# A ternary feed-forward: who clears, who rounds, and when the turned tile is copied

## The chip, the cores and the metric

The kernel runs on one core of a Trainium2 chip. The metric is the time on the device, in microseconds (us), of one execution of the whole program; a median over runs is given.

## The reference, cut to what matters

The program is a decoder of four layers on 2 x 1024 tokens of width 256, twelve sublayers, each `x = layernorm(x + sublayer(x))`. The change touches the third of them, a feed-forward with ternary weights and tokens rounded to eight bits:

```python
def _weight_quant(w):
    scale = 1.0 / jnp.clip(jnp.mean(jnp.abs(w)), 1e-05)
    return jnp.clip(jnp.round(w * scale), -1.0, 1.0) / scale
def _act_quant(x):
    scale = 127.0 / jnp.clip(jnp.max(jnp.abs(x), axis=-1, keepdims=True), 1e-05)
    return jnp.clip(jnp.round(x * scale), -128.0, 127.0) / scale
def _bitlinear(x, w):
    return jnp.einsum('bsi,oi->bso', _act_quant(x), _weight_quant(w))
gate = jax.nn.silu(_bitlinear(x, w_gate))      # 256 -> 1024
up = _bitlinear(x, w_up)                       # 256 -> 1024
return _bitlinear(gate * up, w_down)           # 1024 -> 256
```

The sublayer before it is a masked cross attention over 77 context tokens, the one behind it a paged causal attention.

## The kernel before, in words

Each sublayer is a stage, a block of five instruction streams, one for each engine, written in order by hand and joined by semaphores; all engines meet at a barrier between stages. The tokens are held twice on chip: x_tok with tokens on partitions (16 tiles of 128 tokens) and xT turned.

The ternary stage is `bit_ffn_stage` (L1122). Its start-up: TensorE takes the mean of the absolute weights (summed in the stage before); VectorE makes the scales. Rounding to whole numbers is done by adding a large constant (ROUND, 1.5 x 2^23) and taking it away again. For weights, `weight(n)` on ScalarE does both (L1258 adds, L1260 takes away and casts to bf16), and `clip(n)` on VectorE clips to -1 and 1 (L1335). For tokens, `quant_x(c)` on VectorE takes a group of four tiles: maximum (L1320), m127 (L1322), reciprocal (L1324), four scalings with the constant added (L1330); `quant_x(c)` on ScalarE takes the constant away and casts (L1266); `turn_x(c)` on TensorE turns the group by eight transposes into a half of h_ps; `copy_x(c)` on ScalarE copies it to xqT (L1270). All four groups are done before the loop. sx, the scale of the tokens times that of the weights, is made once for all tiles (L1361).

The loop runs over the 16 tiles n, with two rounds more to run out. TensorE: gate(n+1) into g_ps (L1196), upward(n+1) into u_ps (L1205), downward(n-1) into y_ps (L1222), turn_h(n), eight transposes into h_ps (L1214), and, from round 11 on, a turned tile of the normalized output (`tail.turn`, L3002). ScalarE: silu(n+1) of g_ps (L1276), copy_h(n-1), which takes the constant away from all of h_ps and casts to hqT (L1289), round_h(n), which scales the hidden tile and adds the constant (L1282), and a small scaling; from round 11 on the copy of a turned output tile (L3009). VectorE: hidden(n), which is the product of silu and u_ps (L1342), its maximum (L1344), and two small steps to the scale of the rounding; each second round the residual of two tiles with its statistics (`tail.add`, L2939, L2948, L2952), and at rounds 10, 14, 17 and 18 the norm of the tiles that are ready (L2982). Waits: gate(n+1) needs silu(n) done, upward(n+1) needs the product of hidden(n), turn_h(n) needs round_h(n) and copy_h(n-1), copy_h(n) needs turn_h(n), downward(n) needs copy_h(n).

GpSimd fills v_all, the values of the paged attention (128 x 8192 f32, 4 MB), with zero (L1168), waits, and sets the columns of ones (L1170); later it takes the roots for the norms. The first stage of the program uses v_all's room for products of its own; the second stage, `masked_heads_stage` (L863), does not. In the second stage SyncE's queue issues the loads of the three ternary weights (`bit.load`) and then `clear_outputs`, a DMA that clears 4 MB of token_outputs in the main memory from a tile of zeros; the experts' stages wait for it, far later.

## Time and profile before

| what | us |
|---|---|
| plain runs, median of 3 | 2783.19 (2782.19 to 2787.72) |
| profiled execution | 2797.71 |
| span of its trace | 2795.6 |
| stage before (masked cross attention) | 263.36 to 413.46 |
| ternary stage | 413.46 to 541.99 |
| TensorE busy over the span | 2461.0 (88%) |
| VectorE / ScalarE / GpSimd busy | 1451.2 / 885.6 / 507.1 |

PE is TensorE's products, PEld its weight loads, DVE VectorE, ACT ScalarE, POOL GpSimd, SP SyncE. A timeline row gives the start and the length in us, engine, line, operation, written tile<-read tiles, shapes and count; in square brackets stands how long the engine had been idle before it, and who ended that. A row of several instructions (x4) gives the time from the first to the last. A row of the table of stretches gives from:to, length, the busy time of each engine with its count, TensorE's granted clock as a share of 2.4 GHz, the share of the DMA engines and GB/s. A row of the groups gives count | busy us, mean ns of one | idle us before.

### The profile page before, as it was taken

What the parts mean: (1) busy time and instruction counts of PE and PEld (TensorE: products, weight loads), DVE (VectorE), ACT (ScalarE), POOL (GpSimd) and SP (SyncE); (2) the same over time, 40 slices, a digit from 0 to 9 for tenths busy, and PEclk for the clock granted to TensorE, in tenths of its full rate; (3) what the DMA queues carried; (4) which work ended last, traced back from release to release, by engine and by line L of the source; (5) the groups of instructions that cost most, each with busy time, mean ns of one, the idle gap of its engine ahead of it and who ended that gap; (6) DMA issues with size and microseconds to landing.
All of it is one profiled execution on the core that took longest, in us unless ns stands there. A gap on an engine that the chain in (4) does not pass through costs nothing. (4 is left out here: it accounts for less than half of the span.)

```text
span 2795.6 us, 35763 instructions
## 1 busy us (share of the span) xinstructions
PE 2461.0 (88%) x14243; PEld 1700.6 (61%) x14251; DVE 1451.2 (52%) x2493; ACT 885.6 (32%) x1293; POOL 507.1 (18%) x424
## 2 busy tenths in 40 slices
PE   6887775778888979988999998979999799999888
PEld 4665663432222768865667666756666577777764
DVE  7996876558774440125564564561110355455543
ACT  1111556424556113324432442211221222222132
POOL 3332340040001123420100001112221310001010
PEclk8898887988999979999999999869999899999999
DMA  3002000054330025633322321132231300000000
GB/s 111 1 1 78 29 22 9 8 129 88 63 63 26 14 86 216 236 111 106 96 73 56 95 66 33 30 119 67 100 100 57 107 18 17 12 12 17 1 33 30
DMA packets 73542, 177.23 MB, mean 63 GB/s; under 512 B 16919, under 2 KB 37016, under 8 KB 67833
## 3 DMA queue, kind: packets, MB, share of 16 engines
q1 hardware_dynamic: 60484, 122.54, 15.5%
q0 software_dynamic: 10368, 50.01, 5.3%
q10 hardware_dynamic: 2542, 2.62, 0.3%
q8 instruction: 103, 1.69, 0.3%
q14 instruction: 45, 0.37, 0.0%
HBM read 149.51 MB, written 25.43 MB: 63 GB/s over the span
## 5 line engine op out<-in xcount | busy, mean ns | idle before, releaser
L1623 PE MATMUL L_ffn_h_ps<-L_ffn_xgT,L_ffn_w 128*128 128x512 f32 (+2 forms) x992 | 231.9, 390 | 7.0 <-DVE L_ffn_xgT L1706 3.4
L1635 PE MATMUL L_ffn_y_ps<-L_ffn_w,L_ffn_h 128*128 128x256 f32 x1008 | 222.5, 380 | 4.8 <-issue 3.9
L526 DVE TENSOR_REDUCE L_attn_neg<-L_attn_Y 128x1 f32<-128x512 f32 (+3 forms) x304 | 187.3, 658 | 55.3 <-PE L_attn_Y L399 53.9
L1681 ACT ACTIVATE L_ffn_h<-L_ffn_h_ps,L_ffn_w 128x640 f32<-128x640 f32 (+2 forms) x184 | 101.9, 555 | 346.7 <-PE L_ffn_h_ps L1623 333.4
L1635 PEld LDWEIGHTS L_ffn_y_ps<-L_ffn_w,L_ffn_h 128*128 128x128 f32 x1008 | 189.7, 190 | 33.1 <-issue 8.3
L1623 PEld LDWEIGHTS L_ffn_h_ps<-L_ffn_xgT,L_ffn_w 128*128 128x128 f32 x992 | 154.2, 192 | 84.1 <-issue 66.8
L496 ACT ACTIVATE L_attn_room<-L_attn_Y 128x1024 f32<-128x1024 f32 (+1 forms) x192 | 147.6, 814 | 80.5 <-PE L_attn_Y L450 79.8
L399 PE MATMUL L_attn_Y<-L_attn_K,L_attn_Q 104*128 104x512 bf16 (+3 forms) x384 | 119.5, 362 | 43.4 <-DVE L_attn_neg L526 26.0
L1715 DVE TENSOR_TENSOR L_ffn_yg<-L_ffn_y_ps,L_ffn_w 128x256 f32<-128x256 f32 x63 | 26.8, 425 | 223.5 <-PE L_ffn_y_ps L1635 223.5
L1706 DVE COPY L_ffn_xgT<-L_ffn_t_ps 128x256 f32<-128x256 f32 x63 | 24.6, 421 | 214.2 <-PE L_ffn_t_ps L1610 195.3
L1756 POOL DMA_INDIRECT token_outputs<-L_ffn_yg,puts x63 | 62.0, 984 | 325.6 <-DVE L_ffn_yg L1715 325.6
L2330 PE MATMUL L_attn_X<-xT,L_attn_w 128*128 128x512 f32 x256 | 113.0, 594 | 0.0
L2330 PE MATMUL L_attn_X<-xT,L_attn_first_w 128*128 128x512 f32 x256 | 112.8, 593 | 0.0
L399 PEld LDWEIGHTS L_attn_Y<-L_attn_K,L_attn_Q 104*128 104x128 bf16 x384 | 33.6, 100 | 117.1 <-DVE L_attn_neg L526 95.7
L2878 POOL TENSOR_TENSOR L_attn_prod<-L_attn_k_sum,L_attn_qs 128x1024 f32<-128x1024 f32 x16 | 37.7, 2356 | 347.9 <-DVE L_attn_qs L2852 347.9
L844 POOL TENSOR_TENSOR L_attn_v_all<-L_attn_q,L_attn_kv 128x2048 f32<-128x2048 f32 x16 | 73.9, 4623 | 132.9 <-DVE L_attn_room L802 59.8
L450 PE MATMUL L_attn_Y<-L_attn_Q,L_attn_K 107*128 107x512 bf16 (+3 forms) x384 | 95.9, 335 | 2.0 <-ACT L_attn_room L496 1.9
L2556 POOL TENSOR_TENSOR L_attn_sq_sum<-L_attn_sq_sum,L_attn_sq 128x1024 f32<-128x1024 f32 x14 | 33.0, 2359 | 331.1 <-ACT L_attn_sq L2433 331.1
L2415 ACT ACTIVATE L_attn_bc<-L_attn_bc 128x1024 f32<-128x1024 f32 x32 | 33.9, 1059 | 172.2 <-DVE L_attn_bc L2508 172.2
L435 PE MATMUL L_attn_Y<-L_attn_room,L_attn_v_all 128*32 128x512 f32 (+3 forms) x768 | 83.0, 511 | 0.1
L2330 PEld LDWEIGHTS L_attn_X<-xT,L_attn_w 128*128 128x128 f32 x256 | 47.8, 192 | 53.8 <-issue 53.8
L2330 PEld LDWEIGHTS L_attn_X<-xT,L_attn_first_w 128*128 128x128 f32 x256 | 47.3, 190 | 53.9 <-issue 53.1
(578 smaller groups left out, 5065.7 us busy)
## 6 DMA issues: line engine op xcount, KB each, us to landing
L_ffn_w<-in_L_ffn_w SPq DMA_DIRECT2D x8, 2180.0 KB
L_attn_bc<-decays SPq DMA_DIRECT2D x32, 512.0 KB, 6.1
L_attn_bp<-decays SPq DMA_DIRECT2D x32, 256.0 KB, 6.9
L_attn_Q<-L_attn_q_parts SPq DMA_DIRECT2D x48, 128.0 KB, 4.3
L_attn_K<-L_attn_k_parts SPq DMA_DIRECT2D x48, 128.0 KB, 6.4
L_attn_first_w<-in_L_attn_w SPq DMA_DIRECT2D x8, 640.0 KB
L_attn_w<-in_L_attn_w SPq DMA_DIRECT2D x8, 640.0 KB, 3.9
token_outputs<-zero SPq DMA_DIRECT2D x1, 4096.0 KB, 21.2
```

The costliest lines, as they stand in the source:

```text
L399: mm = nc.tensor.matmul(R[n % 2][:, u * wdt:(u + 1) * wdt], Q[0:KM, par, j0 + u, tt * P:(tt + 1) * P], K[0:KM, par, j0 + u, c * CW:c * CW ...
L435: mm = nc.tensor.matmul(O[32 * j:32 * j + 32, lo:CW], v_all[:, it, gt, 32 * j:32 * j + 32], probs[:, (2 * n + j // 2) % 4, j % 2, lo:CW], ...
L450: mm = nc.tensor.matmul(S[e % 2][:, j % 2, lo:CW], K[0:KS, par, j, gt * P:(gt + 1) * P], Q[0:KS, par, j, tc * CW + lo:(tc + 1) * CW], star ...
L496: nc.scalar.activation(probs[:, e % 4, :, lo:CW], S[e % 2][:, :, lo:CW], ACT.Exp, scale=SCALE).then_inc(exp_done, 1)
L526: nc.vector.tensor_reduce(neg[:, c, j0:j0 + heads, tt], R[n % 2][:, 0:heads * width(tt, c)].rearrange("p (h k) -> p h k", h=heads), X_AXIS ...
L844: nc.gpsimd.tensor_tensor(prod[n % 2][:, h, :, :], q[n % 2][:, h, :].unsqueeze(2).broadcast_to([P, HALF, H, DH]), keys(n).unsqueeze(1).bro ...
L1623: ins = nc.tensor.matmul(h_ps[f % 2][:, lo // CW, 0:hi - lo], w1[g % NB][:, kt, f * P:(f + 1) * P], xgT[u][:, kt, lo:hi], start=kt == 0, s ...
L1635: ins = nc.tensor.matmul(y_ps[k % 2][:], h[:, f, t * P:(t + 1) * P], w2[g % NB][:, f, :], start=f == 0, stop=f == FT - 1)
L1681: nc.scalar.activation(h[:, f, 0:n], h_ps[f % 2][:].rearrange("p c n -> p (c n)")[:, 0:n], func, bias=b1[g % NB][:, f:f + 1]).then_inc(sem ...
L1756: nc.gpsimd.indirect_dma_start(core.outputs, at, yg[g % 2][:, t, :], None).then_inc(y_stored[g % 2], 16)
L2330: ins = nc.tensor.matmul(x[:, c * CW:(c + 1) * CW], w[1 - par][:, kt, r, :], xT[:, kt, b * T + c * CW:b * T + (c + 1) * CW], start=kt == 0 ...
L2878: nc.gpsimd.tensor_tensor(prod[:], k_sum[:], qs[1 - par][:], ALU.mult).then_inc(prod_ready, 1)
```

## The change

Five things. The zeros of v_all are written by a DMA on SyncE's queue in the stage before, between the weights' loads and `clear_outputs`; GpSimd waits for it where it filled. Of each token group, `scale_x` (maximum, m127, reciprocal, and now that group's sx) and `round_x` (scaling with the constant, and the subtraction of it with the cast to bf16) are both on VectorE; group 0 comes before the loop, groups 1 to 3 are spread over rounds 1, 2, 4, 6 and 8; turning and copying them follow in rounds 2, 6 and 10, through x_ps in place of h_ps. For weights, VectorE takes the constant away and clips in two passes. ScalarE's table of silu is loaded by an activation of one column, ahead of the first silu. And copy_h(n-1) stands before silu(n+1), in two halves of four transposes each, each with its own signal.

```diff
@@ masked_heads_stage, sync
             bit.load(sp)
+            flat = values[:].rearrange("p i t n -> p (i t n)").rearrange("p (a n) -> p a n", n=2 * P)
+            sp.dma_start(flat, over(core.zero[:], flat.shape[1])).then_inc(bit.values_cleared, 16)
             clear_outputs(core, sp)
@@ bit_ffn_stage
-        xq_ps = [h_ps[:, 4 * u:4 * u + 4, :].bitcast(BF16).rearrange("p a (b n) -> p (a b n)", b=2) for u in range(2)]
+        xq_ps = x_ps[:].bitcast(BF16)
+        HALF = FT // 2
+        TURN_X = {2: 1, 6: 2, 10: 3}
+        SCALE_X, ROUND_X = {1: 1, 2: 2, 6: 3}, {1: 1, 4: 2, 8: 3}
@@ gpsimd
-            nc.gpsimd.memset(values[:], 0.0).then_inc(v_cleared, 1)
-            pool.wait_ge(v_cleared, 1)
+            pool.wait_ge(weights.values_cleared, 16)
@@ tensor
             def turn_h(n):
                 pe.wait_ge(h_up, n + 1)
-                if n:
-                    pe.wait_ge(hqT_ready, n)
-                for ft in range(FT):
-                    mm = nc.tensor.transpose(h_ps[:, ft, :], hr[n % 2][:, ft * P:(ft + 1) * P], core.ident[:])
-                mm.then_inc(h_turned, 1)
+                for half in range(2):
+                    if n:
+                        pe.wait_ge(hqT_ready, 2 * n - 1 + half)
+                    for ft in range(half * HALF, half * HALF + HALF):
+                        mm = nc.tensor.transpose(h_ps[:, ft, :], hr[n % 2][:, ft * P:(ft + 1) * P], core.ident[:])
+                    mm.then_inc(h_turned, 1)
             def downward(n):
-                pe.wait_ge(hqT_ready, n + 1)
+                pe.wait_ge(hqT_ready, 2 * n + 2)
...
             gate(0)
-            turn_x(1)
             pe.wait_ge(w_clipped, 2)
             upward(0)
-            turn_x(2)
-            turn_x(3)
-            pe.wait_ge(xqT_ready, N // P // QT)
             for n in range(NT_ + 2):
                 if n + 1 < NT_:
                     gate(n + 1)
                     upward(n + 1)
+                if n in TURN_X:
+                    turn_x(TURN_X[n])
@@ scalar
             def copy_h(n):
-                act.wait_ge(h_turned, n + 1)
                 if n >= 4:
                     act.wait_ge(tail.y_mm, (n - 2) // 2)
-                nc.scalar.activation(hqT[n % 2][:], h_ps[:], ACT.Identity, bias=down_[:]).then_inc(hqT_ready, 1)
+                for half in range(2):
+                    act.wait_ge(h_turned, 2 * n + half + 1)
+                    ft = slice(half * HALF, half * HALF + HALF)
+                    nc.scalar.activation(hqT[n % 2][:, ft, :], h_ps[:, ft, :], ACT.Identity, bias=down_[:]).then_inc(hqT_ready, 1)
             weight(0)
-            quant_x(0)
+            weight(1)
             copy_x(0)
-            weight(1)
-            for c in range(1, N // P // QT):
-                quant_x(c)
-                copy_x(c)
-            act.wait_ge(sx_set, 1)
+            nc.scalar.activation(warm[:], core.one[:], ACT.Silu)
             silu(0)
             weight(2)
             for n in range(NT_ + 2):
+                if 1 <= n <= NT_:
+                    copy_h(n - 1)
                 if n + 1 < NT_:
                     silu(n + 1)
-                if 1 <= n <= NT_:
-                    copy_h(n - 1)
+                if n in TURN_X:
+                    copy_x(TURN_X[n])
                 if n < NT_:
                     round_h(n)
@@ vector
+            def scale_x(c):
...
+                for k in range(2):
+                    last = nc.vector.tensor_scalar(sx[:, k, t], m127[:, t], wmean[:, k:k + 1], None, ALU.mult)
+                last.then_inc(sx_set, 1)
+            def round_x(c):
...
+                dve.wait_ge(x_up, c + 1)
+                nc.vector.tensor_scalar(xq[c % 2][:], xr[c % 2][:], -ROUND, None, ALU.add).then_inc(x_down, 1)
             def clip(n):
+                dve.wait_ge(w_up, n + 1)
+                nc.vector.tensor_scalar(wq[n][:], w32[n][:], -ROUND, 1.0, ALU.add, ALU.min).then_inc(w_down, 1)
                 dve.wait_ge(w_down, n + 1)
-                nc.vector.tensor_scalar(wq[n][:], wq[n][:], 1.0, -1.0, ALU.min, ALU.max).then_inc(w_clipped, 1)
+                nc.vector.tensor_scalar(wq[n][:], wq[n][:], -1.0, None, ALU.max).then_inc(w_clipped, 1)
...
-            quant_x(0)
-            quant_x(1)
+            scale_x(0)
+            round_x(0)
             clip(0)
-            quant_x(2)
             clip(1)
-            quant_x(3)
...
             for n in range(NT_ + 2):
                 if n < NT_:
                     hidden(n)
+                if n == 0:
+                    clip(2)
+                if n in SCALE_X:
+                    scale_x(SCALE_X[n])
+                if n in ROUND_X:
+                    round_x(ROUND_X[n])
```

## Rows read from the trace of the kernel before

**Rows 1.** Table of stretches: the stage before, the middle of the loop, everything behind.
```profile
263.36:413.46 150.10, 114.67 (x1264) 95.73 (x1264) 118.61 (x151) 78.25 (x150) 53.40 (x47) 0.86 0.15 50
455.00:510.00 55.00, 39.78 (x247) 23.99 (x251) 41.98 (x80) 36.30 (x43) 1.92 (x2) 1.00 0.00 1
541.99:2795.60 2253.61, 2059.72 (x11753) 1408.36 (x11753) 1029.40 (x1999) 683.87 (x966) 351.83 (x332) 0.94 0.24 71
```

**Rows 2.** Timeline of the ternary stage, its start-up: start us, us, engine, line.
```profile
413.46 6.92 POOL L1168 MEMSET L_attn_v_all<- 128x8192 f32 x1 [2.22 <-POOLq L57]
...
414.30 2.10 ACT L1258 ACTIVATE L_ffn_w<-L_ffn_w,L_ffn_round_up,L_ffn_wscale 128x2048 f32<-128x2048 f32 x1 [0.34 <-DVE L_ffn_wscale L1353]
...
415.40 5.00 DVE L1322 TENSOR_SCALAR L_ffn_m<-L_ffn_amax 128x4 f32<-128x4 f32 x1
...
421.81 1.21 DVE L1320 TENSOR_REDUCE L_ffn_amax<-x_tok 128x4 f32<-128x1024 f32 x1
...
423.47 1.14 DVE L1330 TENSOR_SCALAR L_ffn_xr<-x_tok,L_ffn_ascale 128x256 f32<-128x256 f32 x4
...
424.27 1.01 ACT L1270 COPY L_ffn_xqT<-L_ffn_h_ps 128x1024 bf16<-128x1024 bf16 x1 [1.19 <-PE L_ffn_h_ps L1186]
...
432.67 0.37 DVE L1361 TENSOR_SCALAR L_ffn_sx<-L_ffn_m,L_ffn_wmean 128x16 f32<-128x16 f32 x2
...
438.42 1.28 ACT L1276 ACT_TABLE_LOAD   x1
...
444.95 0.69 DVE L1335 TENSOR_SCALAR L_ffn_wq<-L_ffn_wq 128x2048 bf16<-128x2048 bf16 x1 [11.90 <-ACT L_ffn_wq L1260]
...
445.56 1.28 DVE L1342 SCALAR_TENSOR_TENSOR L_ffn_h<-L_ffn_u_ps,L_ffn_sx,L_ffn_sg 128x1024 f32<-128x1024 f32 x1
...
451.57 1.06 PE L1196 MATMUL L_ffn_g_ps<-L_ffn_wq,L_ffn_xqT 128*128 128x512 bf16 x2
...
453.27 1.81 PE L1205 MATMUL L_ffn_u_ps<-L_ffn_wq,L_ffn_xqT 128*128 128x512 bf16 x4
```

**Rows 3.** Timeline, one round in the middle of the loop.
```profile
470.43 1.11 ACT L1289 ACTIVATE L_ffn_hqT<-L_ffn_h_ps,L_ffn_round_down 128x1024 bf16<-128x1024 f32 x1
...
470.57 1.28 DVE L1342 SCALAR_TENSOR_TENSOR L_ffn_h<-L_ffn_u_ps,L_ffn_sx,L_ffn_sg 128x1024 f32<-128x1024 f32 x1 [2.37 <-ACT L_ffn_sg L1276]
...
471.43 1.24 ACT L1282 ACTIVATE L_ffn_hr<-L_ffn_h,L_ffn_round_up,L_ffn_hscale 128x1024 f32<-128x1024 f32 x1
...
472.72 0.85 PEld L1214 LDWEIGHTS L_ffn_h_ps<-ident,L_ffn_hr 128*128 128x128 f32 x8 [0.36 <-ACT L_ffn_hr L1282]
...
473.41 0.88 DVE L2939 SCALAR_TENSOR_TENSOR x_tok<-L_ffn_y_ps,L_ffn_sh,x_tok 128x256 f32<-128x256 f32 x2
...
474.71 1.12 ACT L1276 ACTIVATE L_ffn_sg<-L_ffn_g_ps,L_ffn_sx 128x1024 f32<-128x1024 f32 x1 [1.86 <-PE L_ffn_g_ps L1196]
...
475.10 0.25 DVE L2952 BATCH_NORM_AGGREGATE L_ffn_tail_mv<-L_ffn_tail_stats 128x2 f32<-128x6 f32 x2
```

**Rows 4.** Timeline, a round with a turned output tile, and the stage's end.
```profile
519.98 1.24 ACT L1282 ACTIVATE L_ffn_hr<-L_ffn_h,L_ffn_round_up,L_ffn_hscale 128x1024 f32<-128x1024 f32 x1
...
521.96 1.37 DVE L2982 TENSOR_SCALAR x_tok<-x_tok,L_ffn_tail_mv,L_ffn_tail_rstd 128x256 f32<-128x256 f32 x4
...
522.84 0.59 ACT L3009 COPY xT<-L_ffn_x_ps 128x512 f32<-128x512 f32 x1 [1.44 <-PE L_ffn_x_ps L3002]
...
533.41 1.12 ACT L1289 ACTIVATE L_ffn_hqT<-L_ffn_h_ps,L_ffn_round_down 128x1024 bf16<-128x1024 f32 x1
...
534.59 0.77 PEld L1222 LDWEIGHTS L_ffn_y_ps<-L_ffn_wq,L_ffn_hqT 128*128 128x128 bf16 x8 [1.93 <-ACT L_ffn_hqT L1289]
...
541.99 0.50 PEld L251 LDWEIGHTS L_attn_Y<-xT,L_attn_room 128*128 128x128 f32 x2 [1.94 <-issue]
```

**Rows 5.** DMA issues of the page: KB, us to landing.
```profile
token_outputs<-zero SPq DMA_DIRECT2D x1, 4096.0 KB, 21.2
```

**Rows 6.** Groups by line and shape on VectorE.
```profile
L2092 DVE TENSOR_SCALAR L_router_hit_all<-L_router_g,L_router_cand 128x1024 bf16<-128x1024 f32 x7 | 5.3, 753 | 0.2
```

More of the change, by code:

```diff
@@ L860, in _, with masked_heads_stage @@
                     tail.shift(pool, g)
-def masked_heads_stage(nc, core, early, bit):
+def masked_heads_stage(nc, core, early, bit, values):
     A = core.A
@@ L1258, in weight @@
                 nc.scalar.activation(w32[n][:], w32[n][:], ACT.Identity, scale=wscale[:, n:n + 1], bias=up[:]).then_inc(w_up, 1)
-                act.wait_ge(w_up, n + 1)
-                nc.scalar.activation(wq[n][:], w32[n][:], ACT.Identity, bias=down_[:]).then_inc(w_down, 1)
-            def quant_x(c):
-                act.wait_ge(x_up, c + 1)
-                if c >= 2:
-                    act.wait_ge(xq_turned, c - 1)
-                nc.scalar.activation(xq[c % 2][:], xr[c % 2][:], ACT.Identity, bias=down_[:]).then_inc(x_down, 1)
             def copy_x(c):
                 act.wait_ge(xq_turned, c + 1)
-                nc.scalar.copy(xqT[:, :, c * QT * P:(c + 1) * QT * P], xq_ps[c % 2].rearrange("p (k n) -> p k n", k=KT)).then_inc(xqT_ready, 1)
+                nc.scalar.copy(xqT[:, :, c * QT * P:(c + 1) * QT * P], xq_ps).then_inc(xqT_ready, 1)
             def silu(n):
                 act.wait_ge(g_mm, n + 1)
+                act.wait_ge(sx_set, n // QT + 1)
                 if n >= 2:
@@ L1327, in quant_x @@
                     dve.wait_ge(x_down, c - 1)
+                    dve.wait_ge(xq_turned, c - 1)
                 for k in range(QT):
@@ L1353, in _ @@
             nc.vector.reciprocal(wscale[:], wmean[:]).then_inc(w_scaled, 1)
-            quant_x(0)
-            quant_x(1)
+            scale_x(0)
+            round_x(0)
             clip(0)
-            quant_x(2)
             clip(1)
-            quant_x(3)
-            for k in range(2):
-                last = nc.vector.tensor_scalar(sx[:, k, :], m127[:], wmean[:, k:k + 1], None, ALU.mult)
-            last.then_inc(sx_set, 1)
-            dve.wait_ge(sx_set, 1)
-            clip(2)
             for n in range(NT_ + 2):
@@ L3050, in __init__ @@
         self.summed = nc.alloc_semaphore("L0_ffn_w_summed")
+        self.values_cleared = nc.alloc_semaphore("L0_ffn_values_cleared")
     def load(self, sp):
```

15 lines of the change are left out of this document (7 added, 8 removed).

## The prediction, made before the changed kernel ran

> **What bounds the kernel now.** I read the table of stretches first, then the timeline of the stage that the change touches, line by line. TensorE is busy for 2059.7 of the 2253.6 us behind this stage [rows 1], and nothing is changed there; what counts is how much earlier the ternary feed-forward ends. The stage runs from 413.46 us [rows 2] to 541.99, where the first product of the next stage begins. The reader is to see three parts in it.
>
> Start-up, 413.46 to 445.56, where VectorE begins the first gated product, "hidden(0)" [rows 2]. TensorE isn't the limit here. GpSimd's fill of v_all takes 6.92 us and ends at 420.38; VectorE's two-step operation on four numbers (L1322) begins at 415.40 and ends at 420.40, 5.00 us, though the whole group of maximum, L1322 and reciprocal takes 421.81 to 423.47 = 1.66 us once the fill is over. So the fill holds it up by some 4.8 us. After that ScalarE does everything: all casts, all copies, a table load of 1.28 at 438.42, the third weight; VectorE stands idle for 11.90 us until its clip at 444.95 [rows 2].
>
> The loop, one token tile per round. Starts on ScalarE show the round: silu 474.71, copy of the turned tile 1.01 later (as each 128x1024 step passes on after about 1.0: copy 470.43, rounding 471.43), rounding 1.00 later, TensorE's turn of h 1.29 after the rounding's start (472.72), next silu 1.99 later. 1.01 + 1.00 + 1.29 + 1.99 = 5.29 us [rows 3]. It is a ring through ScalarE and TensorE; VectorE's part of it (hidden 470.57, next operation 473.41: 2.84) isn't in the ring. Output tiles turned from unit 11 on make it longer.
>
> The end: after the last copy (533.41) the down product follows at 534.59, and the next stage 7.40 after that [rows 4].
>
> **Part 1: the clear by DMA.** The fill goes; GpSimd waits for a DMA issued at the start of the stage before, which lasts 150 us [rows 1]. The nearest row is the clear of token_outputs, also 4 MB, from the same zero tile: 21.2 us to landing, behind 3 MB of weights [rows 5]. Bounds: nothing, or, if writing into the on-chip memory were twice as slow, some 45 us, which still ends 100 us before the feed-forward. It delays the clear behind it, which nobody wants before the experts. I take 0. If the cover were gone, GpSimd would wait, and behind it only the ones and the roots of the norm, first needed near 475. Gain on the path: 4.8 us, in the start-up below.
>
> **Part 2: start-up.** VectorE passes 415.40 as before. Then m127 and reciprocal 1.66 - 1.25 = 0.41 (the maximum's 1.21 and 0.04 of hand-over), two scalings of sx 0.34 (0.37 measured for 16 columns), four roundings 1.14 and a wait of 0.05, and the subtraction. The last, f32 to bf16, 128x1024, isn't done by this stage now; the same form elsewhere takes 0.75 [rows 6], and the other bound is the maximum's full-rate 1.21 [rows 2]. I take 0.75, since kind of operation and shapes are the same. 415.40 + 0.41 + 0.34 + 1.19 + 0.75 = 418.09. ScalarE's copy follows a finished cast by 1.19 and takes 1.01: 420.29; gate(0) 420.4. I leave TensorE at 1.2 GHz there, as it is in these rows now (512 columns in 0.43 us): gate to upward 453.27 - 451.57 = 1.70, upward 1.81 [rows 2].
> The clips: f32 to bf16 over 2048 columns plus a second pass, which is today's 0.69 and passes on after 0.61 [rows 2]. First pass: twice 0.75 less one fixed part, 1.4 (bounds 1.3 and 2.4); 2.04 each. Clip(0) ends at 420.1, clip(1) at 422.2; ScalarE has the two weights scaled by 414.30 + 2 x 2.10 = 418.5. So upward(0) starts at 422.2, not 422.1, and hidden(0) at 422.2 + 1.81 + 0.1 = 424.1. The table load is done ahead, between 420.3 and the silu at 422.5; without that cover it would cost 1.3. Start-up gains 445.56 - 424.1 = 21.5 us.
>
> **Part 3: what bounds the loop afterwards.** The copy now stands before the silu. The ring then has no copy in it: rounding 1.29, turn and gate 1.99, silu 1.01 = 4.29, and the half copies fit while gate works. But VectorE has taken on work and becomes the bound of units 0 to 10. Its sum from hidden(0) to hidden(11) [rows 2 to 4, 6]:
> 11 x hidden 2.84 = 31.2; clip(2) 2.0; three scale_x at 1.66 + 0.34 = 6.0; three round_x at 1.19 + 0.75 - 0.07 (overlap) = 5.6; four residual additions with statistics, 473.41 to 475.35 less 0.08 overlap, 1.86 each = 7.4; the norm of eight tiles, 2 x 1.37 - 0.1 = 2.6. Together 54.9 us, 4.99 a unit, under 5.29 but well over 4.29. The waits in between hold: from the end of hidden(n-1) the ring needs 1.29 + 1.99 + 1.15 (1.01 and 470.57 - 470.43) = 4.43 us to hidden(n+1), and VectorE has 2.84 plus the extra steps of two units, at least 3.7, to do in that time. The copies of turned tokens (1.0 each, three times) fall in this slack of 2.1 us. Were they to stick out, they would cost 1.0 each.
>
> From unit 11 the extra steps end and the turned output tiles begin, so ScalarE is the bound. From a rounding's start: output tile's copy 519.98 to 522.84 = 2.86, then that copy 0.59 less 0.11 overlap, two half copies, silu 1.01. A half copy of 128x512: between the 0.48 of the 128x512 output copy and half of 1.00 plus a whole fixed part, 0.65; I take 0.57, the 0.48 plus what a biased activation takes over a copy at 1024 columns (1.11 against 1.01). Round: 2.86 + 0.48 + 1.14 + 1.01 = 5.49. In the rest, hidden(11) to its scale 2.92; three rounds 16.5; from rounding 14 to rounding 15 without a silu 4.48; then 2.86 + 0.48, the second half 0.57 later, its 0.68 and 0.06 of hand-over to the down product (1.31), and 7.40. Sum from hidden(0): 54.9 + 2.9 + 16.5 + 4.5 + 12.0 = 90.8 us against 541.99 - 445.56 = 96.4 now [rows 2, 4]. Gain 5.6.
>
> The half copies are the one edit with a price: as a whole the copy passed on after 1.00, in halves after 1.14. The Trainium skill (ScalarE: Activation LUTs, What ACT_TABLE_LOAD costs) gives a biased ACTIVATE 280 ns + 0.833 ns a column, 93 ns of it overlapped with the next: 1.13 whole, which agrees with the 1.11 of the row, and 2 x 0.61 for the halves. By it each late round would be 0.09 longer and the whole gain smaller by an estimated 0.4 us.
>
> **Sum.** 21.5 + 5.6 = 27.1 us. The profiled execution took 2797.71 us (span 2795.6), the median of the plain runs is 2783.19, 14.5 less; I carry the difference over unscaled: 2756.1 us, and 2770.6 under the profiler.
>
> **Rivals.**
> (a) The loop gives nothing. VectorE's sum needs only 5.6 us more, 0.47 for each of the 12 extra steps before hidden(11), and each holds a wait on its own engine, which I cost at 0.03 to 0.05. Against: the rows of the group 421.81 to 423.47 hold three such waits already. Gain 21.5: 2761.7.
> (b) The converting operations run at full rate, not double: 0.46 + 2 x 1.0 in the start-up, 1.0 + 3 x 0.46 in the loop, 4.8 together. Gain 22.3: 2760.9. The same number comes out if the 5.00 us of L1322 isn't the fill's doing, which the two ends within 0.02 us speak against.
> (c) Slower: TensorE never gets to 2.4 GHz in this stage. Its work is then the bound: gate and upward 1.70 each [rows 2], turn twice the 0.85 of [rows 3], and as much for down, also eight products: 6.8 a unit. hidden(15) comes at 424.1 + 15 x 6.8 + 8 for turned tokens and output tiles = 534, the end 4.5 + 12 and some 3 for the slower products later, 554: 12 us late, 2795. It decides where the granted clock is near 0.5 for most of the loop. For it: 512 columns still take 0.43 us at 453, with idle gaps at each wait [rows 2]. Against: 1.00 over 455 to 510 with TensorE busy for 39.8 of 55 us [rows 1], and the new loop has less idle time for the same work. The Trainium skill (TensorE: Matmul & The Clock Gate, Part 1) holds that half rate is the default and that activity releases it; gaps speak for this rival, but by that rule, too, the denser loop should stay at the upper level, and the trace agrees for the present gaps.
> (d) The stages behind run at another mean clock: 0.01 of the 0.94 there is 2059.7 x 0.0106 = 22 us [rows 1]. It has no sign; the plain runs lie within 5.5 us of each other, so I give it a few us at both ends.
>
> **Chances.** The forecast 0.74, its own range 2751 to 2761 (unknown costs: conversions, half copies, 0.5 us of clock in the start-up, and (d)); (a) 0.10; (b) with its twin 0.08; (c) 0.03; (d) as the decider 0.05. The range takes in (a) and (b) and 5 us of drift: 2749 to 2768. About 0.2%, 5.6 us, is what can be told from no change. Faster 0.93, within 0.04, slower 0.03.
>
> **What would show it.** Right: L1322's successor takes 0.17 us; the first hidden starts near 424; VectorE idles hardly at all between then and hidden(11), near 479; rounds of about 5.0 there, 5.5 from unit 11; the turned tile's copies of about 0.68 us each; the next stage starts near 515. Wrong: the subtraction near 1.2; VectorE idle in the first eleven units (then the ring or TensorE's order bounds); granted clock at 0.5 behind 430; or a next stage that starts near 515 while the total isn't 27 us shorter, which would put the difference behind this stage.

## The result, and the profile after

| comparison | kernel before, us | changed kernel, us | ratio, 95% interval |
|---|---|---|---|
| first | 2785.28 (2782.19 to 2794.69) | 2768.39 (2764.22 to 2772.95) | 0.9934, 0.9913 to 0.9955 |
| second | 2786.29 (2778.60 to 2796.22) | 2762.27 (2760.21 to 2770.25) | 0.9915, 0.9890 to 0.9939 |
| third | 2789.60 (2783.97 to 2797.12) | 2759.37 (2754.66 to 2760.80) | 0.9891, 0.9875 to 0.9907 |

The change makes the kernel faster, by 0.7 to 1.1 per cent: by 16.9 us in the comparison that the prediction is held against, by 24.0 and 30.2 in two later ones. The forecast was 27.1. The profiled execution took 2769.68 us (span 2767.9) against 2797.71 and 2795.6: 28.0 and 27.7 less. Times are medians.

The table of stretches of the changed kernel: the stage before, the whole ternary stage, as much of its loop as rows 1 show, everything behind the stage.

```profile
263.02:413.30 150.28, 114.98 (x1264) 96.08 (x1264) 118.63 (x151) 78.33 (x150) 53.46 (x47) 0.86 0.23 78
413.30:514.06 100.76, 68.18 (x442) 43.62 (x450) 83.68 (x178) 74.91 (x98) 5.62 (x9) 0.94 0.06 21
425.00:480.00 55.00, 41.64 (x278) 26.80 (x284) 53.22 (x109) 44.10 (x59) 1.93 (x2) 1.00 0.00 1
514.06:2767.90 2253.84, 2060.84 (x11753) 1410.76 (x11753) 1028.09 (x1999) 682.63 (x966) 351.77 (x332) 0.94 0.24 71
```

The stage runs from 413.30 to 514.06. It ends 27.93 us earlier than before, and what lies behind takes 2253.84 us where it took 2253.61 [rows 1]: in these two traces all of the gain is made in the stage and all of it stays. In 55 us of the loop TensorE is busy for 41.64 us, where it was for 39.78 [rows 1], and VectorE for 53.22, where it was for 41.98. The stage before takes 150.28 us with the second clear in it and took 150.10 [rows 1]. The clear of v_all is issued at 264.34 and lands 22.0 us later, 127 us ahead of the ternary stage: its cover holds, as forecast.

The start-up, beside rows 2:

```profile
414.14 4.08 ACT L1260 ACTIVATE L_ffn_w<-L_ffn_w,L_ffn_round_up,L_ffn_wscale 128x2048 f32<-128x2048 f32 x2 [0.35 <-DVE L_ffn_wscale L1359]
...
415.24 0.17 DVE L1317 TENSOR_SCALAR L_ffn_m<-L_ffn_amax 128x4 f32<-128x4 f32 x1
...
416.95 0.69 DVE L1334 TENSOR_SCALAR L_ffn_xq<-L_ffn_xr 128x1024 bf16<-128x1024 f32 x1
417.56 1.22 DVE L1338 TENSOR_SCALAR L_ffn_wq<-L_ffn_w 128x2048 bf16<-128x2048 f32 x1
...
418.84 1.01 ACT L1264 COPY L_ffn_xqT<-L_ffn_x_ps 128x1024 bf16<-128x1024 bf16 x1 [0.62 <-PE L_ffn_x_ps L1190]
...
420.68 0.69 DVE L1340 TENSOR_SCALAR L_ffn_wq<-L_ffn_wq 128x2048 bf16<-128x2048 bf16 x1
...
421.65 1.91 PE L1208 MATMUL L_ffn_u_ps<-L_ffn_wq,L_ffn_xqT 128*128 128x512 bf16 x4
...
423.71 1.28 DVE L1348 SCALAR_TENSOR_TENSOR L_ffn_h<-L_ffn_u_ps,L_ffn_sx,L_ffn_sg 128x1024 f32<-128x1024 f32 x1 [2.34 <-PE L_ffn_u_ps L1208]
```

GpSimd no longer fills; VectorE's two-step operation takes 0.17 us where it took 5.00 [rows 2]. The subtraction (L1334) takes 0.69, a weight's first pass 1.22 and its second 0.69. ScalarE has scaled two weights by 418.22 and then waits for the turned tokens. The first gated product starts at 423.71, 10.4 us after the stage's start, where it was 32.1 [rows 2].

Two units in the middle of the loop, beside rows 3. The first ends with a residual addition (L2944 and its statistics), the second with a group's rounding (L1331, L1334):

```profile
442.23 0.88 DVE L2944 SCALAR_TENSOR_TENSOR x_tok<-L_ffn_y_ps,L_ffn_sh,x_tok 128x256 f32<-128x256 f32 x2
...
444.11 1.28 DVE L1348 SCALAR_TENSOR_TENSOR L_ffn_h<-L_ffn_u_ps,L_ffn_sx,L_ffn_sg 128x1024 f32<-128x1024 f32 x1
...
444.83 1.27 ACT L1286 ACTIVATE L_ffn_hqT<-L_ffn_h_ps,L_ffn_round_down 128x512 bf16<-128x512 f32 x2 [0.56 <-PE L_ffn_h_ps L1218]
...
446.13 1.11 ACT L1271 ACTIVATE L_ffn_sg<-L_ffn_g_ps,L_ffn_sx 128x1024 f32<-128x1024 f32 x1
...
446.98 1.14 DVE L1331 TENSOR_SCALAR L_ffn_xr<-x_tok,L_ffn_ascale 128x256 f32<-128x256 f32 x4
...
448.15 0.69 DVE L1334 TENSOR_SCALAR L_ffn_xq<-L_ffn_xr 128x1024 bf16<-128x1024 f32 x1
...
448.76 1.28 DVE L1348 SCALAR_TENSOR_TENSOR L_ffn_h<-L_ffn_u_ps,L_ffn_sx,L_ffn_sg 128x1024 f32<-128x1024 f32 x1
```

VectorE is never idle in these rows: 442.23 to 444.11 is the addition, 1.88 us, and from the hidden tile at 444.11 to the next it is 4.65. ScalarE is the one that waits now. The copy of the turned tile (L1286, two halves) comes at 444.83, ahead of the silu at 446.13.

A late round and the end, beside rows 4:

```profile
486.45 1.26 ACT L1277 ACTIVATE L_ffn_hr<-L_ffn_h,L_ffn_round_up,L_ffn_hscale 128x1024 f32<-128x1024 f32 x1
...
489.32 0.59 ACT L3014 COPY xT<-L_ffn_x_ps 128x512 f32<-128x512 f32 x1 [1.44 <-PE L_ffn_x_ps L3007]
...
489.80 1.27 ACT L1286 ACTIVATE L_ffn_hqT<-L_ffn_h_ps,L_ffn_round_down 128x512 bf16<-128x512 f32 x2
...
490.95 1.12 ACT L1271 ACTIVATE L_ffn_sg<-L_ffn_g_ps,L_ffn_sx 128x1024 f32<-128x1024 f32 x1
...
491.95 1.25 ACT L1277 ACTIVATE L_ffn_hr<-L_ffn_h,L_ffn_round_up,L_ffn_hscale 128x1024 f32<-128x1024 f32 x1
...
514.06 0.50 PEld L251 LDWEIGHTS L_attn_Y<-xT,L_attn_room 128*128 128x128 f32 x2 [1.95 <-issue]
```

From rounding to rounding 5.50 us: 2.87 to the output tile's copy, 0.48, then 1.15 for the two halves and 1.00 for the silu. ScalarE isn't busy throughout: 1.44 of the 2.87 are its wait for TensorE's turn of the output tile. It is the order of its queue that makes the round.

The groups of both kernels over their stages show the two waits that the change removes. Columns: busy us, mean ns of one, then the idle time before them and who ended it. Before:

```profile
L1342 DVE SCALAR_TENSOR_TENSOR L_ffn_h<-L_ffn_u_ps,L_ffn_sx,L_ffn_sg 128x1024 f32<-128x1024 f32 x16 | 20.5, 1284 | 20.5 <-ACT L_ffn_sg L1276 16.7 <-PE L_ffn_u_ps L1205 3.8
...
L1276 ACT ACTIVATE L_ffn_sg<-L_ffn_g_ps,L_ffn_sx 128x1024 f32<-128x1024 f32 x16 | 17.8, 1115 | 23.1 <-PE L_ffn_g_ps L1196 23.1
```

and after:

```profile
L1348 DVE SCALAR_TENSOR_TENSOR L_ffn_h<-L_ffn_u_ps,L_ffn_sx,L_ffn_sg 128x1024 f32<-128x1024 f32 x16 | 20.5, 1281 | 5.8 <-ACT L_ffn_sg L1271 2.8 <-PE L_ffn_u_ps L1208 2.3 <-issue 0.7
L1286 ACT ACTIVATE L_ffn_hqT<-L_ffn_h_ps,L_ffn_round_down 128x512 bf16<-128x512 f32 x32 | 20.3, 687 | 7.4 <-PE L_ffn_h_ps L1218 7.4
...
L1271 ACT ACTIVATE L_ffn_sg<-L_ffn_g_ps,L_ffn_sx 128x1024 f32<-128x1024 f32 x16 | 17.9, 1116 | 0.7 <-PE L_ffn_g_ps L1199 0.5
```

Silu waited 23.1 us for the gate products and waits 0.7; VectorE's wait ahead of the hidden tile fell from 20.5 to 5.8, which lies in the first unit and in the late ones.

### The profile page after: what moved, and what is told of

Same layout as the page of the kernel before. It is cut to its first block and busy times, and to the rows that moved or that the text cites. A ratio compares the mean times of both kernels' runs of the same rounds, so it can differ in the third digit from the quotient of the medians.

```text
span 2767.9 us, 35799 instructions
## 1 busy us (share of the span) xinstructions
PE 2455.5 (89%) x14243; PEld 1701.9 (61%) x14251; DVE 1450.8 (52%) x2506; ACT 877.6 (32%) x1303; POOL 500.1 (18%) x423
## 5 line engine op out<-in xcount | busy, mean ns | idle before, releaser
L1628 PEld LDWEIGHTS L_ffn_h_ps<-L_ffn_xgT,L_ffn_w 128*128 128x128 f32 x992 | 154.9, 193 | 83.9 <-issue 67.8
L2335 PEld LDWEIGHTS L_attn_X<-xT,L_attn_first_w 128*128 128x128 f32 x256 | 47.3, 190 | 53.9 <-issue 53.1
## 6 DMA issues: line engine op xcount, KB each, us to landing
L_attn_Q<-L_attn_q_parts SPq DMA_DIRECT2D x48, 128.0 KB, 4.2
L_attn_K<-L_attn_k_parts SPq DMA_DIRECT2D x48, 128.0 KB, 6.3
```

The lines of the kernel that those rows point to most:

```text
L1628: ins = nc.tensor.matmul(h_ps[f % 2][:, lo // CW, 0:hi - lo], w1[g % NB][:, kt, f * P:(f + 1) * P], xgT[u][:, kt, lo:hi], start=kt == 0, s ...
L2335: ins = nc.tensor.matmul(x[:, c * CW:(c + 1) * CW], w[1 - par][:, kt, r, :], xT[:, kt, b * T + c * CW:b * T + (c + 1) * CW], start=kt == 0 ...
```

## The experiments

Stages are compared from traces: "the stage" is the time from its first operation on VectorE (wmean) to the first weight load of the next stage. It is 128.10 us in the profiled kernel before and 128.01 in a second trace of it, 100.33, 100.34 and 100.34 in three of the changed one; so 0.2 us mean something there, where the medians leave some 5 open. The medians rest on 2 (no early table load) to 12 executions. Diffs are against the changed kernel unless it is said otherwise.

| kernel | stage | behind it | median | ratio, interval |
|---|---|---|---|---|
| before, repeated | 128.0 | 2250.1 | 2781.31 | 0.9994, 0.9976 to 1.0011 |
| before + clear by DMA | 124.5 | 2237.4 | 2777.89 | 0.9988, 0.9974 to 1.0003 |
| silu ahead of the copy | 111.7 | 2256.2 | 2777.14 | 0.9968, 0.9952 to 0.9983 |
| fill on GpSimd again | 105.6 | 2252.3 | 2771.53 | 0.9946, 0.9927 to 0.9965 |
| groups ahead of the loop | 105.5 | 2252.3 | 2772.89 | 0.9934, 0.9914 to 0.9953 |
| rebalanced | 102.7 | 2244.8 | 2754.53 | 0.9898, 0.9877 to 0.9918 |
| changed, second | 100.3 | 2247.3 | 2762.27 | 0.9915, 0.9890 to 0.9939 |
| changed, third | 100.3 | 2244.4 | 2759.37 | 0.9891, 0.9875 to 0.9907 |
| no early table load | 100.3 | 2247.5 | 2758.20 | 0.9891, 0.9871 to 0.9910 |
| copy in one piece | 99.8 | 2251.2 | 2764.14 | 0.9913, 0.9890 to 0.9936 |
| output tiles on VectorE | 98.7 | 2248.8 | 2762.29 | 0.9902, 0.9886 to 0.9918 |

Three chips took part. On one (median of the kernel before: 2786.29) ran the changed kernel for the second time, the fill, the copy in one piece and the silu; on another (2781.86) the kernel before repeated, the clear alone, the rebalanced one and the pause below; on a third (2789.60) the rest.

**The changed kernel again**, no edit.

> The changed kernel once more, unaltered. In its trace the next stage starts 27.9 us earlier than before (514.06 against 541.99), and its profiled execution is 28.0 us shorter, but its plain runs have a median only 16.9 us below that of before. Theory A (sampling: the stages behind vary by several us from run to run, whatever the kernel): over another five rounds the difference goes towards 27.7, ratio near 0.990. Theory B (the stages behind are really slower by some 9 us in the changed kernel, and the profiled execution of before was a slow one of its kind): the ratio stays near 0.9935. Stage end near 514.1 under both.

The stage is the same to 0.1 us; the total is 6.1 us lower than in the first comparison, and of the two traces it is the part behind the stage that is shorter, 2247.3 against 2253.8. The ratio, 0.9915, lies between the two theories.

**The fill back on GpSimd.**

```diff
-            sp.dma_start(flat, over(core.zero[:], ...
-            pool.wait_ge(weights.values_cleared, 16)
+            nc.gpsimd.memset(values[:], 0.0).then_inc(weights.values_cleared, 1)
+            pool.wait_ge(weights.values_cleared, 1)
```

> The changed kernel with one part undone: GpSimd fills v_all with zero at the start of the ternary stage again, and no DMA clears it. Theory (the fill blocks VectorE's two-step operation on four numbers until it ends, and start-up is a chain through it): that operation takes 5.0 us again, hidden(0) comes 4.8 us later, near 428.5, the next stage starts near 518.9. Rival (the scaling of the weights on ScalarE covers part of it, or the slack of the loop takes it back): less than 3 us. A second rival: the 4 MB clear in the stage before costs something there or behind, then the total rises by less than the stage does.

```profile
413.74 5.00 DVE L1316 TENSOR_SCALAR L_ffn_m<-L_ffn_amax 128x4 f32<-128x4 f32 x1
```

The four numbers take 5.00 us again and the first hidden tile comes 4.83 us later, as forecast. The stage is 5.3 longer; the other 0.45 is the last turn of an output tile, 1.11 us instead of 0.66, with TensorE at the lower clock. The maximum over x_tok just ahead (414.02 to 415.21 in the changed kernel, the same 1.19 under the fill) isn't held up. The Trainium skill (SBUF — State Buffer, Who interferes with whom) says that VectorE's two-port modes and GpSimd lock each other out of a shared pair of ports for a whole instruction, and that the reduction has no such mode; the rows agree with both, as far as durations can: the operation ended within 0.02 us of the fill [rows 2]. That ports are the cause no row shows. Nor was every VectorE operation held up: the scaling of three numbers from y_ps at 413.89, in the kernel before, took 0.16 us with the fill running since 413.46.

**The copy in one piece.**

```diff
-                for half in range(2):
...
+                nc.scalar.activation(hqT[n % 2][:], h_ps[:], ACT.Identity, bias=down_[:]).then_inc(hqT_ready, 1)
```

> The changed kernel with the turned tile copied whole, in one piece, still ahead of the silu. Theory (VectorE bounds units 0 to 10, ScalarE the rest, where a copy in two halves passes on after 1.15 us and a whole one after 1.00): no change up to hidden(11), then 0.15 us shorter rounds, next stage 0.7 us earlier, near 513.4. Rival (the halves are what lets copy and gate overlap, the ring would be the bound without them): rounds longer by 0.3 to 0.5 us, stage end 2 to 6 us later.

The late rounds take 5.36 us instead of 5.50, the stage 99.75 instead of 100.33: the halves cost 0.6 us and bring nothing.

**Silu ahead of the copy**, as before, in the otherwise changed loop.

```diff
-                if 1 <= n <= NT_:
-                    copy_h(n - 1)
                 if n + 1 < NT_:
                     silu(n + 1)
+                if 1 <= n <= NT_:
+                    copy_h(n - 1)
```

> The changed kernel with the order on ScalarE undone: silu(n+1) ahead of copy_h(n-1), which keeps its halves. Theory (the order takes the copy out of the ring): the ring is 1.01 + 1.15 + 1.29 + 1.99 = 5.44 us again, above VectorE's 4.95 a unit, and the three copies of turned tokens, 1.0 each, stick out; 60 us to hidden(11) against 54, late rounds 5.9 against 5.5, the end 1.0 later: next stage near 522, 8 us later. Rival (VectorE is the bound of the first eleven units either way): only the late part, 2.5 us.

```profile
440.84 1.11 ACT L1271 ACTIVATE L_ffn_sg<-L_ffn_g_ps,L_ffn_sx 128x1024 f32<-128x1024 f32 x1 [1.86 <-PE L_ffn_g_ps L1199]
...
441.85 1.26 ACT L1286 ACTIVATE L_ffn_hqT<-L_ffn_h_ps,L_ffn_round_down 128x512 bf16<-128x512 f32 x2
...
446.28 1.11 ACT L1271 ACTIVATE L_ffn_sg<-L_ffn_g_ps,L_ffn_sx 128x1024 f32<-128x1024 f32 x1 [1.87 <-PE L_ffn_g_ps L1199]
```

The ring of rows 3 is back, with 1.14 for the halves in it: from silu to silu 5.44 us, and 1.87 us of idle time ahead of each for the gate product. From the first hidden tile to the last it is 83.9 us instead of 74.0. The order is the dearest single part: 11.4 us of the stage, where 8 were expected: 4.5 up to hidden(11), 5.5 from there to hidden(15), 1.5 behind. The late rounds themselves are 5.88, as expected; the surprise is the step from hidden(11) to hidden(12), 7.92 us against 4.71. The copy of the last token group stands in it, and TensorE, which waited for 0.99 us ahead of the turn of h, fell to the lower level: the granted clock was 0.57 from 484 to 488, and four gate products took 1.91 us, not 1.03. This fall and a slower last turn (0.97 us, not 0.66) are some 1.9 of the 11.4 us, an estimate from the starts of these operations in both traces.

**The kernel before, repeated**, no edit.

> The kernel before, unaltered, for a second trace. The first trace of before has 2253.6 us behind the ternary stage; its 19 plain runs, less the stage's end at 542.0, have a median of 2242. Theory B (the stages behind take some 8 us less in before than in all kernels of the changed kind, whose medians are 2249 to 2252): this trace has 2235 to 2248 us behind, and a stage by stage comparison shows where. Theory A (they don't differ): 2247 to 2256, as the traces so far. Stage itself: 128.1 us from its start under both.

Its stage is 128.0 us and 2250.1 lie behind it, where the first trace had 2253.6: theory A. But its profiled execution, 2794.44, is the slowest of its eight, 13.1 above their median.

**The clear by DMA alone**, in the kernel before.

```diff
+            sp.dma_start(flat, over(core.zero[:], ...
             clear_outputs(core, sp)
...
-            nc.gpsimd.memset(values[:], 0.0).then_inc(v_cleared, 1)
+            pool.wait_ge(weights.values_cleared, 16)
```

> The kernel before with one part of the change alone: v_all cleared by a DMA in the stage before, GpSimd waiting for it. Theory: the two-step operation on four numbers takes 0.17 us, not 5.00, everything that hangs on it comes 4.8 us earlier, and as the start-up is a chain through it the next stage starts 4.8 us earlier, 123.3 us from the stage's start, not 128.1. Rival (in the old order ScalarE's casts, copies and weights bound the start-up, so that VectorE's earlier hand-over is partly lost): 2 to 4 us. On the stages behind: if the clear is what makes them longer, about 2250 us; if not, 2242.

```profile
416.42 2.00 ACT L1260 ACTIVATE L_ffn_wq<-L_ffn_w,L_ffn_round_down 128x2048 bf16<-128x2048 f32 x1
...
418.33 1.13 ACT L1266 ACTIVATE L_ffn_xq<-L_ffn_xr,L_ffn_round_down 128x1024 bf16<-128x1024 f32 x1
```

The stage gains 3.6 us and not 4.8, and all of it by the first hidden tile. The scaled tokens are there at 416.96, but ScalarE, which rounds them in this kernel, is at the first weight's two passes until 418.4. What the fill costs depends on who waits next: 3.6 with ScalarE behind it, 4.8 with VectorE.

**A pause behind the stage**, 24 times 128x1024 set to zero on VectorE, each waiting for the one before, in the changed kernel.

```diff
         sublayers[n]()
+        if n == EARLY_UNTIL:
+            idle_stage(nc, core, 24)
```

> The changed kernel with a pause between the ternary stage and the next: VectorE clears a scratch tile 24 times one after another, some 26 us with the barrier a bit more, all other engines idle. So the stages behind begin about where they begin in the kernel before. Theory A (what lies behind doesn't depend on when it begins): total up by the pause, 26 to 29 us, against the changed kernel, behind 2249 as now. Theory B' (it does, through what the chip did before: a denser 100 us buys a lower granted clock later): behind falls to 2242 and the total rises by only some 20.

The next stage starts at 542.1, as late as in the kernel before, and 2238.4 us lie behind it; the median of eleven executions is 2784.18, ratio 1.0012 (0.9996 to 1.0029). A twelfth, of 4887.1 us, is left out; what happened in it isn't known. This was meant to show whether the stages behind depend on when they begin. On the same chip the kernel before, whose next stage starts at 542.5, had 2250.1 behind it. The same start with 11.7 us between them: the start time alone isn't what sets it. Taken by itself 2238.4 is nearer to the 2242 of theory B' than to the 2249 of theory A, and the granted clock behind the stage is 0.95, where the kernel before has 0.94 on this chip. Against B', the rebalanced kernel has no pause, ran on this chip too, and gave nothing back: a gain of 27.3 us in the medians from a stage 25.4 shorter. One trace can't settle it. The pause is 542.1 less the 512.6 at which this stage ends without it, 29.5 us; taken off the median it leaves 2754.7, a gain of 27.2 on this chip.

**Rebalanced**: whole copy, the constant of groups 1 to 3 taken away on ScalarE, six output tiles copied by VectorE.

```diff
+            def take_x(c):
...
+                nc.scalar.activation(xq[c % 2][:], xr[c % 2][:], ACT.Identity, bias=down_[:]).then_inc(x_down, 1)
...
+                    nc.vector.tensor_copy(core.xT[:, :, g * 2 * P:(g + 1) * 2 * P], x_ps[:]).then_inc(tail.x_copied, 1)
```

> The changed kernel with three more alterations: the turned tile copied whole; the constant taken away from token groups 1 to 3 by ScalarE in the rounds where they are turned; the first six turned output tiles copied to xT by VectorE behind hidden(n+1). Theory (VectorE bounds units 0 to 10, ScalarE the rest): three times 0.62 us off VectorE's sum, so hidden(11) 1.9 us earlier; late rounds without the 0.48 copy and with a whole copy 4.7 to 5.0 us, not 5.5; stage about 4 to 5 us shorter, 95.5 to 96.5 us from start to the next stage against 100.4. Rival (the ring through ScalarE is close behind VectorE, and 1.05 us more on it in three rounds sticks out): no gain before hidden(11), 2 us in all.

```profile
476.89 1.15 ACT L1265 ACTIVATE L_ffn_xq<-L_ffn_xr,L_ffn_round_down 128x1024 bf16<-128x1024 f32 x1
...
478.75 1.01 ACT L1269 COPY L_ffn_xqT<-L_ffn_x_ps 128x1024 bf16<-128x1024 bf16 x1 [0.71 <-PE L_ffn_x_ps L1190]
...
479.66 1.24 ACT L1282 ACTIVATE L_ffn_hr<-L_ffn_h,L_ffn_round_up,L_ffn_hscale 128x1024 f32<-128x1024 f32 x1
```

It failed: 102.7, longer by 2.4. In the rounds that take a group, ScalarE takes the constant away (1.15), waits 0.71 for TensorE's turn, copies (1.01), and only then rounds h; from the hidden tile at 478.24 to the one at 484.35 it is 6.11 us, where the changed kernel has 4.71. hidden(11) comes 0.9 us later and not 1.9 earlier. Its plain median, 2754.53, is the lowest of all, of four executions and on another chip than the changed kernel: the median doesn't rank the stages.

**The changed kernel, a third time**, no edit.

> The changed kernel as it is, a third time against the kernel before. Theory A (the stage gives 27 to 28 us, the stages behind it are untouched, and what a comparison shows beside that is their run to run drift): the plain medians lie 17 to 28 us apart, ratio 0.990 to 0.994, and the profiled execution, whatever its total, has the next stage 100.2 to 100.6 us behind the stage's first scale. Rival B (the earlier end is given back in the stages behind, a fixed 8 to 10 us): the medians lie 15 to 19 us apart again, and from the next stage to the end of the span there are at least 8 us more than in the kernel before.

The stage is 100.34 us and 2244.4 lie behind it, 9 less than in the first trace of the kernel before, where rival B wanted at least 8 more: it fails. The medians lie 30.2 us apart and the ratio is 0.9891, both just outside what theory A allowed, so its drift was put too low.

**Four output tiles on VectorE**, whole copy, tokens as in the changed kernel.

```diff
+                    if g > 3:
+                        tail.copy(act, g)
...
+                    if g < 4:
...
+                        nc.vector.tensor_copy(core.xT[:, :, ...
```

> The changed kernel with the turned tile copied whole, and with the first four turned output tiles (rounds 11 to 14) copied by VectorE behind the hidden tile of the round after; tokens as in the changed kernel. Theory: the late rounds are bound by ScalarE, 5.51 us, of which the output tile's copy is 0.48 and the split of the turned tile's copy 0.14; four rounds without the first and the whole copy's 0.14 in each would be 4.9, so from the first hidden tile to the last some 72.3 instead of 74.0 us, and the stage 98.5 to 99.2 instead of 100.4. Rival (as in the rebalanced kernel, VectorE's waits on the turned tiles delay its last additions and norms): the last hidden tile early, the end not, stage 99.8 or more. Second rival (the late rounds' limit is VectorE's own additions and norms): 5.3 to 5.5 us a round as before, stage 99.8.

```profile
486.66 1.23 ACT L1276 ACTIVATE L_ffn_hr<-L_ffn_h,L_ffn_round_up,L_ffn_hscale 128x1024 f32<-128x1024 f32 x1
...
487.94 1.09 PE L1217 MATMUL L_ffn_h_ps<-ident,L_ffn_hr 128*128 128x128 f32 x8 [0.60 <-ACT L_ffn_hr L1276]
...
488.87 0.60 PE L3009 MATMUL L_ffn_x_ps<-ident,x_tok 128*128 128x128 f32 x4
...
489.13 1.11 ACT L1283 ACTIVATE L_ffn_hqT<-L_ffn_h_ps,L_ffn_round_down 128x1024 bf16<-128x1024 f32 x1 [1.06 <-PE L_ffn_h_ps L1217]
...
489.31 1.03 PE L1199 MATMUL L_ffn_g_ps<-L_ffn_wq,L_ffn_xqT 128*128 128x512 bf16 x4
...
490.37 1.11 ACT L1270 ACTIVATE L_ffn_sg<-L_ffn_g_ps,L_ffn_sx 128x1024 f32<-128x1024 f32 x1
...
491.39 1.23 ACT L1276 ACTIVATE L_ffn_hr<-L_ffn_h,L_ffn_round_up,L_ffn_hscale 128x1024 f32<-128x1024 f32 x1
```

From the first hidden tile to the last 72.4 us instead of 74.0, the stage 98.7: the theory, to 0.1 us. The roundings of the late rounds are 4.73 apart, and that is the ring again, with TensorE's turn of the output tile in it: 1.28 from the rounding to the turn of h, 0.93 to the output tile's turn, 0.44 to the gate products, 1.06 to the silu, 1.02 to the next rounding. VectorE, with additions, norms and the copies, has hardly any slack left either: from the hidden tile at 486.85 to the one at 496.87 it isn't idle. Against it the rebalanced kernel is 3.3 us longer up to hidden(15), by the tokens' move to ScalarE, and 0.7 behind it, by the last two copies. By the stage this is the best version of all; its 1.7 us over the changed kernel are too little for the medians to show.

**No early table load.**

```diff
-            nc.scalar.activation(warm[:], core.one[:], ACT.Silu)
```

> The changed kernel without the activation of one column that loads ScalarE's table ahead. The load of 1.28 us then stands between the end of gate(0) and silu(0). Theory: the table load isn't hidden by anything else, but the product waits for upward(0) as well, which ends about 0.1 us after the silu; hidden(0) comes 1.2 us later and the stage takes 101.6 instead of 100.4. Rival 1 (the load is issued ahead of the wait for gate(0), so that it costs nothing by itself): stage within 0.3 of 100.4. Rival 2: in the loop no slack gives any of it back, so that the whole 1.28 stays to the end; the half of it or less that stays would say that the loop takes it up.

```profile
417.32 1.28 ACT L1271 ACT_TABLE_LOAD   x1
...
419.36 1.11 ACT L1271 ACTIVATE L_ffn_sg<-L_ffn_g_ps,L_ffn_sx 128x1024 f32<-128x1024 f32 x1 [0.75 <-PE L_ffn_g_ps L1199]
```

Rival 1 holds. The load is an instruction of its own, ahead of the wait of silu(0): it begins as soon as the copy has ended, and it has ended 0.75 us before gate(0) has. The one-column activation is worth nothing; what hid the load was ScalarE's idle time, which the start-up now has.

**Groups 1 to 3 ahead of the loop.**

```diff
-        TURN_X = {2: 1, 6: 2, 10: 3}
-        SCALE_X, ROUND_X = {1: 1, 2: 2, 6: 3}, {1: 1, 4: 2, 8: 3}
+        TURN_X, SCALE_X, ROUND_X = {}, {}, {}
...
+            for c in range(1, 4):
+                scale_x(c)
...
```

> The changed kernel with token groups 1 to 3 scaled, rounded, turned and copied before the loop, as the kernel before does, instead of spread over rounds 1 to 10. Theory (VectorE's sum bounds the first eleven rounds): hidden(0) comes later by three groups of 1.66 + 0.34 + 1.19 + 0.70 = 3.9, 11.7 us, and the loop up to hidden(11) is short of the same 11.6 less what the ring doesn't let through: the ring is 4.3 to 4.4 us a round, so 11 rounds take 47.5 to 48.5 instead of 53.9, and the stage is 100.4 + 11.7 - 5.9 = 106.2 (105.5 to 107). Rival (the ring with the copy ahead of the silu has no faster round than 4.9, VectorE isn't what bounds it): 53 to 54 us for eleven rounds and a stage of 111 to 112. Second rival: VectorE's remaining work, additions and the norm, 2.84 + 0.93 a round, sets 4.0 and the ring's 4.3 is wrong: below 46 us, stage below 104.5.

```profile
441.64 1.28 DVE L1351 SCALAR_TENSOR_TENSOR L_ffn_h<-L_ffn_u_ps,L_ffn_sx,L_ffn_sg 128x1024 f32<-128x1024 f32 x1 [2.48 <-ACT L_ffn_sg L1272]
...
445.94 1.28 DVE L1351 SCALAR_TENSOR_TENSOR L_ffn_h<-L_ffn_u_ps,L_ffn_sx,L_ffn_sg 128x1024 f32<-128x1024 f32 x1 [1.37 <-ACT L_ffn_sg L1272]
```

The first hidden tile is 8.3 us later and not 11.7: 10.7 us of VectorE's work are added, but 2.34 of them fall into its wait for upward(0). The eleven rounds take 50.3 us instead of 53.9. The eight of them from 441.64 to 476.38 take 4.34 each, and VectorE waits for silu again (2.48 and 1.37 in the rows): that is the ring, forecast at 4.29. The last, 5.41, has the norm of eight tiles in it. The first two are slow, 4.73 and 5.40, with gate's products at the lower clock (1.91 us for four of 512 columns, against 1.03 from 443 on). Net 5.1 us worse (0.45 of it again the last turn). The stage of 105.5 was forecast at 106.2, and partly by luck: the part before the loop came out 3.4 us shorter than forecast, the loop some 2.3 longer. So VectorE is what bounds the first eleven rounds of the changed kernel, and spreading the groups pays because in the loop they fill the gaps that VectorE has here ahead of each hidden tile.

## Why the prediction was right about the stage and high on the gain

Each step against its own time, from the stage's start:

| step | forecast | measured |
|---|---|---|
| L1322's successor | 0.17 | 0.17 |
| subtraction, 128x1024 | 0.75 | 0.69 |
| a weight's two passes, one after the other | 2.04 | 1.9 |
| start-up gained (to the first hidden tile) | 21.5 | 21.7 |
| first hidden tile to hidden(11) | 54.9 | 53.9 |
| late round | 5.49 | 5.50 |
| two half copies | 1.14 | 1.15 |
| loop and end gained | 5.6 | 6.1 |
| next stage starts | 514.9 | 514.06 |
| profiled execution | 2770.6 | 2769.68 |

**Start-up.** Right in size and in mechanism. The clips are what upward(0) waits for, as forecast, and end at 421.37 instead of 422.2: they start 0.5 us earlier, and each pass is a little shorter. The fill's share, 4.8 us, is 4.83 in the changed kernel. The price of the table load without its cover, 1.3, was right for the duration, but the cover was put down to the early load, and the run without it shows that the idle time alone does it.

**Loop.** That VectorE takes the ring's place up to unit 11 and ScalarE from there is shown from both sides: with the groups taken out the ring appears at 4.34, with the output tile's copy taken out of ScalarE's queue the late rounds fall from 5.50 to 4.73. VectorE's sum was 1.0 us too large: scale_x passes on after 1.79 where 2.00 stood (its two scalings are 0.24 long, not 0.34), three times; the subtractions and clip(2) make up the rest. Behind hidden(11) the sum was 0.6 too small, most of it in the first late round, 5.81 us and not 5.49. The two errors work against each other, so that the 6.1 looks closer to the 5.6 than the terms are. The Trainium skill's figure (ScalarE: Activation LUTs, What ACT_TABLE_LOAD costs), by which a half copy passes on after 0.61, gives 1.22 for two; the rows have 1.15 to the silu. The measurement decides, though both are near.

**Rivals.** (a) and (b) fall with the rows: the loop gave 6.1, the converting operations run at 0.69 and 1.22. (c) falls: the granted clock was 0.61 from 412 to 425 and 1.00 from there to 455; four products of 512 columns took 1.91 us at 421.65 and 1.04 at 425.05. (d), the stages behind, is what was left.

**Where it was off: the carry from one trace to the medians.** The step that failed is "I carry the difference over unscaled" with "I give it a few us at both ends". The trace gave what was forecast, 2769.68 against 2770.6. But the 14.5 us by which the profiled execution of the kernel before lay above its median are no fixed price of the profiler: in the changed kernel they are 1.3, and in the other twelve traces between -2.0 and 13.1. In the first comparison the medians lie 16.9 us apart, 10.2 less than forecast, and 2768.39 is 12.3 above the forecast and 0.4 above the top of the range. The prediction named what that would mean: a next stage near 515 with a total that isn't 27 us shorter puts the difference behind this stage. There nothing is changed, and the fourteen traces have between 2237.4 and 2256.2 us there. The two ends of that on TensorE, in rows of stretches, the clear alone and the silu ahead of the copy:

```profile
538.30:2775.70 2237.40, 2047.16 (x11753) 1399.55 (x11753) 1029.57 (x1999) 681.92 (x966) 351.31 (x332) 0.94 0.24 71
```

and

```profile
524.50:2780.70 2256.20, 2059.37 (x11753) 1409.79 (x11753) 1030.10 (x1999) 682.03 (x966) 351.13 (x332) 0.94 0.24 71
```

The number of instructions is the same; TensorE's busy time is 12.2 us apart, of 18.8 in all, and VectorE's 0.5. So most of it is in the speed of TensorE's products, spread over two milliseconds. The clock in these rows is rounded to 0.94 in both, but each execution's mean granted clock is known to three figures, and the times follow it. Of 19 executions of the kernel before on one chip the fastest took 2778.60 us at 0.937, the slowest 2796.22 at 0.929. Over the 144 executions whose clock is on record, the one of 4887.1 us left out, each against the mean of its own kernel and comparison, the correlation is -0.79 and 0.001 of the clock goes with 1.3 us; the medians of the changed kernel, 2768.39, 2762.27 and 2759.37, have median clocks of 0.930, 0.934 and 0.9355. This is rival (d)'s mechanism, as far as a correlation shows it, at 13 us for 0.01 where (d) had 22. What sets the clock of an execution is not shown.

Whether an early end is given back there is open. Against it: with before and after paired as in the prediction 2253.6 and 2253.8 us lie behind the stage, and 2244.4 in the comparison with a gain of 30.2. The gains of the changed kernel are 16.9, 24.0, 27.2 (the pause taken off) and 30.2, and the stage's 27.7 lies within them. For it: on the chip of the second comparison all four kernels gained less in the median than in the stage, by 3.7 to 7.7 us. On the other two chips it went both ways, from 5.9 less to 3.7 more. Why two comparisons of the same pair are 13 us apart, more than the interval of either, is not settled beyond the clock; no run here tells the chip from the hour.

Rival (d) should have been sized from this kernel's own three plain runs, which were 5.5 us apart and lay 14.5 below their own profiled execution; from that ten us of drift were to be expected, not a few.

## What to carry to other kernels

Find the ring: follow one round from releaser to releaser, and ask which of its members needn't be in it. A copy whose result the ring doesn't need yet costs its full length when it stands in it, between two steps that the ring does need; here moving it ahead of the silu, into the time in which the engine waited anyway, is worth 11.4 us, twice the fill.

Work that moves to another engine is priced by where that engine has gaps, not by its length: 10.7 us of token work cost 8.3 ahead of the loop and 3.6 spread over it, and the subtraction of three groups, 0.69 each on VectorE, cost 3.3 us in all on ScalarE, where it stood between a wait and the rounding. And a gain of one per cent in one stage is read from the stage's own start and end, because the untouched rest drifts by more than the parts of the change are worth; where only totals can be had, the mean granted clock beside each says how much of a difference may be drift.
